# Expert rows in three pieces of 128, and part of the scan's products with C on GpSimd

## The chip, the cores and the metric

The kernel runs on one core of a Trainium2 chip. The metric is the device time of one execution in microseconds (us). The engines are TensorE (PE in the profile, its weight loads PEld), VectorE (DVE), ScalarE (ACT), GpSimd (POOL) and SyncE (SP), which only issues DMAs here.

## The reference

The input is x, 8 sequences of 512 tokens of width 128. Two layers follow, each of the form `x + s * silu(g)` on a normalised x: s comes from an attention-like branch, g from a mixture of experts. In layer 0, s is a Mamba block and g a top-2 mixture of 24 experts in 4 groups of 1024 tokens, each expert taking at most 86 tokens of a group, two matrices deep (128 to 512, layer norm, relu, 512 to 128). In layer 1, s is an attention with 8 heads and g a top-2 mixture of 128 experts. The change touches layer 0 only. Its scan, cut to what matters:

```
h = exp(dt*A) * h + dt * B * x          # per token, 256 channels x 16 states
y = sum over states of (h * C)          # then + x*D, * silu(z), out projection
disp = dispatch(tokens to experts)      # 24 experts x 4 groups x 86 places
h1 = disp @ W1 + b1 ; r = relu(layer_norm(combine(h1)))
out = combine(dispatch(r) @ W2 + b2)
```

## The kernel before, in words

The scan stage (`scan_stage`, about 120 to 800 us of the span) runs the scan and, beside it on the same engines, both expert matrices of layer 0 (`Moe0Experts`). There are 64 steps `i`: 8 sequences b, and in each 8 pairs q of states (q = i mod 8). A step handles two states j = 0, 1 of both channel halves h for 512 tokens.

Each engine has its own instruction stream, in program order, with semaphores between them. In step i:

- VectorE: `times_b(i,0)`, `times_c(i-1,0)`, `times_b(i,1)`, `times_c(i-1,1)`: four products of 128x1024, each of a tensor in SBUF (u, or the states `st`) with one row of B or C that TensorE has broadcast over all partitions into a PSUM bank. Then two scans (L672), one for each channel half, both inputs in SBUF. After the scans, in some steps: `split_rest` (q=0), `split_low` (q=1), four softplus operations (q=3 and 6, L617 to L623), and in q=1 `gate` between the products.
- TensorE: broadcasts the rows (L501) into the three banks of `p_bc`, used in rotation, so that a broadcast waits for whoever used the row three places earlier. It sums the states (`sum_states`, L532, 8 transposes that accumulate in PSUM), once after the product of state 0 and once after that of state 1. `times_b(i+1,0)` on VectorE waits for both sums of step i-1 (the semaphore `hc_used`), since it writes over those states (a ring of four).
- ScalarE: `decays`, four exponentials a step (L444), two for each channel half.

The experts' work is laid between these by slots: each stream is a Python generator, and `side_by_side` lets the scan's stream run to its next `yield`, then the experts' stream to its next. Before the change TensorE has 4 slots in a step (5 in uneven odd ones), ScalarE and VectorE 2. Slots carry three phases in order. In the first, an expert's token rows are gathered by GpSimd (`gather_x`, L1270, one indirect DMA for each group of 96 rows), turned by TensorE, multiplied by W1 (L1361, one piece of 96 rows to a slot), copied out by ScalarE (L1433, and L1423 for the turned rows) and stored. In the second, 16 units of two token tiles are gathered back, combined, normed and weighed; GpSimd's two operations of `weigh` (L1300, L1302) wait for the end of the scans of a chosen step. In the third, rows of r are gathered (L1310), turned (L1409), copied by ScalarE (L1539), multiplied by W2 (L1396) and stored. The pieces of one expert are its 4 groups, padded from 86 to 96 rows: 96 pieces in phases one and three each. GpSimd does not take part in the scan and its stream is not tied to the steps.

TensorE's slot waits for ScalarE's copy of the piece two before it, and ScalarE's slot waits for TensorE's piece of the same slot.

The routing ahead of the scan (`Routing0`) makes the table of rows with 64 small matmuls (L1047), one set for each group, for which VectorE waits (L1147).

Of the kernel before, what the change touches and what calls it, by code (L numbers as in the profile page):

```python
# [38 lines left out]
CP = 96  # L39

# [266 lines left out]
PE_SLOTS, ACT_SLOTS, DVE_SLOTS = 4, 2, 2  # L307

EVEN_FROM, EVEN_TO, FIRST_WINDOW = 22, 43, 26


def uneven(i):

    return not EVEN_FROM <= i < EVEN_TO


def scan_stage(nc, w, xT, z, spare, beside):
# [6 lines left out]
    with ExitStack() as ctx:  # L326
# [14 lines left out]
        st = s.sb("st", [P, RS, 2, L])  # L341
        p_bc = s.ps("p_bc", [P, 3, L])
# [20 lines left out]
        row_used = s.sem("row_used")  # L363
        hc_used = s.sem("hc_used")
# [9 lines left out]
        def b_row(i, j):  # L374

            return 4 * i + 2 * j

        def c_row(i, j):

            return 4 * i + 2 * j + 5  # L380

        rows_in_order = sorted([b_row(i, j) for i in range(STEPS) for j in range(2)] +
                               [c_row(i, j) for i in range(STEPS) for j in range(2)])

        def rows_to(k):

            return sum(1 for n in rows_in_order if n <= k)

        def scalar_steps(act):
# [8 lines left out]
            def copy_hi(b):  # L398
                act.wait_ge(xp_ready, b + 1)
                if b >= 2:  # L400
                    act.wait_ge(row_ready, rows_to(c_row(PAIRS * (b - 1) - 1, 1)))
                nc.scalar.activation(bc3[:, b % 2, :], p_x[0:96, :], ACT.Copy).then_inc(hi_copied, 1)
# [6 lines left out]
            def softplus_logs(b, h):  # L409
# [10 lines left out]
                nc.scalar.activation(logs[:, 1, :], logs[:, 0, :], ACT.Ln, bias=1.0).then_inc(ln_ready, 1)  # L420

# [29 lines left out]
            for i in range(STEPS):  # L451
# [11 lines left out]
                if i % 4 == 3 and uneven(i) or i == EVEN_FROM - 2:  # L463
                    yield
# [12 lines left out]
        def tensor_steps(pe):  # L477
# [20 lines left out]
            def broadcast(k, b, n):  # L498
                if rows_to(k - 3):
                    pe.wait_ge(row_used, rows_to(k - 3))  # L500
                nc.tensor.matmul(p_bc[:, k % 3, :], w["sel"][:, n * P:(n + 1) * P], bc3[:, b % 2, :], start=True,  # L501
                                 stop=True).then_inc(row_ready, 1)

            def broadcast_b(i, j):
# [3 lines left out]
                broadcast(b_row(i, j), b, 2 * q + j)  # L508

            def broadcast_c(i, j):  # L510
                b, q = divmod(i, PAIRS)
                broadcast(c_row(i, j), b, DS + 2 * q + j)
# [11 lines left out]
            def sum_states(i, j):  # L524
# [4 lines left out]
                pe.wait_ge(row_used, rows_to(c_row(i, j)))  # L529
# [26 lines left out]
            for i in range(STEPS):  # L556
                b, q = divmod(i, PAIRS)
                if i:
                    broadcast_c(i - 1, 1)
                if b + 1 < B:  # L560
# [19 lines left out]
                yield  # L580
                yield
                if i % 2 and uneven(i):
                    yield
                if i == EVEN_FROM - 2:
                    yield
                    yield
# [6 lines left out]
        def vector_steps(dve):  # L593
# [37 lines left out]
            def times_b(i, j):  # L631
                b, q = divmod(i, PAIRS)
                k = b_row(i, j)
                dve.wait_ge(row_ready, rows_to(k))
# [3 lines left out]
                if m >= RS and j == 0:  # L638
                    dve.wait_ge(hc_used, m - RS + 2)
                nc.vector.tensor_tensor(st[:, m % RS:m % RS + 2, j, :], u[:, b % 2, :, :],  # L640
                                        p_bc[:, k % 3, :].unsqueeze(1).broadcast_to([P, HALF, L]),
                                        ALU.mult).then_inc(row_used, 1)

            def times_c(i, j):
                m = 2 * i % RS
                k = c_row(i, j)
                dve.wait_ge(row_ready, rows_to(k))
                dve.wait_ge(scanned, 2 * i + 2)
                states = st[:, m:m + 2, j, :]
                nc.vector.tensor_tensor(states, states, p_bc[:, k % 3, :].unsqueeze(1).broadcast_to([P, HALF, L]),  # L650
# [6 lines left out]
            for i in range(STEPS):  # L657
# [7 lines left out]
                if i:  # L665
                    times_c(i - 1, 1)
                yield
                dve.wait_ge(row_used, rows_to(b_row(i, 1)))
# [14 lines left out]
                yield  # L683
                if i % 4 == 3 and uneven(i) or i == EVEN_FROM - 2:
                    yield
# [11 lines left out]

        @block.gpsimd
        def _(pool):
            for _ in beside.pool(pool):  # L700
                pass
# [263 lines left out]
class Routing0:  # L965
# [5 lines left out]
    def __init__(self, nc, ctx, w, r, xnT, p_n, spare):  # L971
# [21 lines left out]
        self.tabf = s.sb("tabf", [CP, HG, E0])  # L993
        self.p_l = s.ps("p_l", [P, 2, 512])
        self.p_t = s.ps("p_t", [CP, 512])
# [22 lines left out]
    def tensor(self, pe):  # L1018
# [24 lines left out]
        for h in range(HG):  # L1043
            for i in range(steps):
                t = i * HG + h
                for k in range(2):
                    ins = nc.tensor.matmul(p_t[:, h * 2 * E0:(h + 1) * 2 * E0], self.A[k][:, t, :],  # L1047
                                           self.R[k][:, t, :, :].rearrange("p a b -> p (a b)"),
                                           start=(i == 0 and k == 0), stop=(i == steps - 1 and k == 1))
# [25 lines left out]
    def vector(self, dve):  # L1075
# [53 lines left out]
        link(v.scalar_tensor_tensor(out=rows[:, :, :], in0=idx[:, :, :], scalar=float(CP), in1=loc[:, :, :],  # L1129
# [15 lines left out]
        pt = self.p_t[:, 0:HG * 2 * E0].rearrange("p (h a c) -> p h a c", h=HG, a=2)  # L1145
# [10 lines left out]
class Moe0Experts:  # L1156
# [13 lines left out]
    def __init__(self, nc, ctx, w, r, arena, xn_dram, W1, y1_dram, r_dram, W2, y2_dram, gathered):  # L1170
        self.nc, self.w, self.r = nc, w, r
        self.xn_rows = xn_dram.rearrange("p t d -> (p t) d")
        self.y1_dram, self.y1_rows = y1_dram, y1_dram.rearrange("h e c n -> (h e c) n")
# [9 lines left out]
        self.xg = first.sb("xg", [CP, 4, HG, D])  # L1183
        self.xgT = first.sb("xgT", [P, 2, HG * CP])
        self.out1 = first.sb("out1", [CP, 2, HG, HID])
# [3 lines left out]
        self.rg = second.sb("rg", [CP, 3, HG, HID])  # L1189
        self.rT = second.sb("rT", [P, 3, FC * CP])  # L1190
        self.out2 = second.sb("out2", [CP, 2, HG, D])
# [34 lines left out]
    def sync(self, sp):  # L1226

        for e in range(E0 + 1):
            if e < E0:
                if e >= 3:  # L1230
                    sp.wait_ge(self.piece_made, 5 * (e - 2))
                sp.dma_start(self.w1[:, e % 3, :], self.W1[e]).then_inc(self.w1_in[e % 3], 16)
            if e:
                f = e - 1
                sp.wait_ge(self.piece_read, 5 * (f + 1))
# [1527 lines left out]
```

## Time and profile before

| | |
|---|---|
| median of 3 runs | 1465.71 us (1464.28 to 1469.84) |
| span of the profiled execution, first to last instruction | 1465.0 us |
| TensorE, VectorE, ScalarE, GpSimd busy | 87%, 84%, 58%, 45% of the span |
| scan stage: scans, products with B, with C | 287.3, 154.3, 154.9 us of VectorE |
| indirect DMAs of phases one, two, three on GpSimd | 119.6, 90.9, 121.5 us |

The profiled execution's span is 0.7 us below the median of the runs; no other time of that execution is given. A row of a group names line, engine, operation, output and inputs, count, then busy time and mean nanoseconds of one, then the idle time of the engine ahead of it and what ended that. A row of a timeline gives start, duration, engine, line and operation; x2 means that two instructions in a row are merged. Records of one engine overlap a little at their ends, so the spacing of starts is the cost of one in a sequence.

### The profile page before, as it was taken

The numbers are of one execution on the slowest core, as the hardware profiler recorded it, in microseconds if no ns is written. First come the engines' busy times: TensorE is split into PE (matmuls) and PEld (weight loads), VectorE is DVE, ScalarE is ACT, GpSimd is POOL, SyncE is SP. The second block draws the span as 40 slices with busy tenths as digits, with TensorE's granted clock in tenths as the row PEclk, the third lists the DMA queues.
The fourth block names the chain that finished last, engine by engine and source line by source line (L and its number), as shares of the span: only waits on it lengthen the run. The fifth ranks groups of instructions, "written<-read, shape, count | busy, mean of one in ns | idle before, by whom it ended". The sixth has DMA issues, their size and how long they took to land. (4 is left out here: it accounts for less than half of the span.)

```text
span 1465.0 us, 21638 instructions
## 1 busy us (share of the span) xinstructions
PE 1277.5 (87%) x7304; PEld 888.3 (61%) x7304; DVE 1227.2 (84%) x2515; ACT 856.9 (58%) x2077; POOL 661.9 (45%) x612
## 2 busy tenths in 40 slices
PE   6977888897887976899897895599999999999997
PEld 5533444453433444788887774467676777777776
DVE  6678999998999899999997778869988555568877
ACT  5357757665798885556654658554464444444462
POOL 0018555605489855664751775339600322147300
PEclk9997999999999877999999898699999999999999
DMA  6003545545244422454552520300020233113201
GB/s 230 1 21 87 147 128 147 141 122 153 82 126 126 123 87 68 126 155 135 146 146 72 190 53 13 119 7 1 2 59 1 60 89 107 41 38 49 25 16 43
DMA packets 75747, 127.50 MB, mean 87 GB/s; under 512 B 11486, under 2 KB 38334, under 8 KB 75030
## 3 DMA queue, kind: packets, MB, share of 16 engines
q1 hardware_dynamic: 56182, 75.24, 17.0%
q0 software_dynamic: 19456, 50.88, 13.2%
q8 instruction: 59, 0.97, 0.3%
q14 instruction: 50, 0.41, 0.1%
HBM read 85.71 MB, written 40.37 MB: 86 GB/s over the span
## 5 line engine op out<-in xcount | busy, mean ns | idle before, releaser
L672 DVE TENSOR_TENSOR_SCAN sc_st<-sc_dA,sc_st 128x1024 f32<-128x1024 f32 x128 | 287.3, 2284 | 0.0
L2164 DVE COPY at_pT<-at_p_t 128x512 f32<-128x512 f32 (+1 forms) x192 | 109.0, 598 | 107.8 <-PE at_p_t L2046 107.4
L1270 POOL DMA_INDIRECT g_state<-xn_scratch,moe_tab x96 | 119.6, 1246 | 174.3 <-POOLq L99 102.4
L2059 PEld LDWEIGHTS at_p_o<-at_V,at_pT 128*128 128x128 f32 x1280 | 154.4, 194 | 31.1 <-issue 30.8
L444 ACT ACTIVATE sc_dA<-sc_dt,g_state 128x511 f32<-128x511 f32 x256 | 168.9, 710 | 7.2 <-DVE sc_st L672 5.3
L650 DVE TENSOR_TENSOR sc_st<-sc_st,sc_p_bc 128x1024 f32<-128x1024 f32 x128 | 154.9, 1211 | 13.4 <-PE sc_p_bc L501 13.2
L640 DVE TENSOR_TENSOR sc_st<-sc_u,sc_p_bc 128x1024 f32<-128x1024 f32 x128 | 154.3, 1206 | 6.6 <-PE sc_p_y L532 6.3
L1310 POOL DMA_INDIRECT g_state<-r_scratch,moe_tab x96 | 121.5, 1266 | 83.6 <-PE e_bank L1409 56.7
L2059 PE MATMUL at_p_o<-at_V,at_pT 128*128 128x128 f32 x1280 | 155.0, 277 | 3.6 <-DVE g_state L2153 3.6
L2026 PE MATMUL at_p_s<-att_xaT,at_qT 128*128 128x512 f32 (+3 forms) x512 | 150.7, 437 | 0.0
L501 PE MATMUL sc_p_bc<-sc_bc,mamba_sel 96*128 96x512 bf16 x256 | 104.9, 411 | 50.5 <-DVE sc_st L640 48.6
L2106 ACT ACTIVATE at_pr<-at_pr,at_nmx 128x512 f32<-128x512 f32 (+3 forms) x256 | 140.1, 551 | 13.3 <-DVE at_nmx L2138 13.1
L532 PEld LDWEIGHTS sc_p_y<-g_ident,sc_st 128*128 128x128 f32 x1024 | 126.9, 148 | 28.6 <-issue 16.3
L532 PE MATMUL sc_p_y<-g_ident,sc_st 128*128 128x128 f32 x1024 | 142.1, 285 | 0.8 <-DVE sc_st L650 0.7
L2094 ACT ACTIVATE at_V<-at_p_q 128x512 f32<-128x512 f32 x58 | 34.6, 596 | 163.3 <-PE at_p_q L2014 163.3
L2138 DVE CUSTOM_DVE_ANT_0 at_pr<-at_p_s,l_mask_wide 128x512 f32<-128x512 f32 (+3 forms) x256 | 111.4, 485 | 11.7 <-PE at_p_s L2026 11.4
L1280 POOL DMA_INDIRECT g_state<-y_scratch,moe_back x64 | 90.9, 1421 | 66.9 <-DMA y_scratch<-g_state 43.8
L2026 PEld LDWEIGHTS at_p_s<-att_xaT,at_qT 128*128 128x128 f32 x512 | 83.0, 191 | 52.8 <-issue 31.8
L1361 PE MATMUL e_bank<-g_state 128*96 128x512 f32 x192 | 100.7, 626 | 9.9 <-ACT g_state L1423 9.9
L2332 POOL DMA_INDIRECT f_xg<-xn_scratch,l_tab x32 | 30.3, 946 | 171.4 <-DVE l_tab L2540 85.1
L1396 PE MATMUL e_bank<-g_state 128*96 128x128 f32 x768 | 101.5, 275 | 4.4 <-ACT g_state L1530 4.0
L2046 PEld LDWEIGHTS at_p_t<-g_ident,at_pr 128*128 128x128 f32 x640 | 75.2, 141 | 39.3 <-DVE at_pT L2164 26.6
(304 smaller groups left out, 2615.0 us busy)
## 6 DMA issues: line engine op xcount, KB each, us to landing
y_scratch<-g_state SPq DMA_DIRECT2D x24, 768.0 KB, 5.2
g_state<-W SPq DMA_DIRECT2D x48, 256.0 KB, 5.5
r_scratch<-g_state SPq DMA_DIRECT2D x16, 512.0 KB, 3.6
y_scratch<-g_state SPq DMA_DIRECT2D x24, 192.0 KB, 2.8
xn_scratch<-g_state SPq DMA_DIRECT2D x16, 256.0 KB, 4.9
g_state<-x SPq DMA_DIRECT2D x4, 512.0 KB, 7.5
g_state<-xn_scratch SPq DMA_DIRECT2D x8, 256.0 KB, 5.2
g_state<-x SPq DMA_DIRECT2D x1, 2048.0 KB, 12.7
```

The costliest lines, as they stand in the source:

```text
L444: ins = nc.scalar.activation(dA[:, m % 4, j, 1:L], dt[:, b % 2, h, 1:L], ACT.Exp, scale=negA[:, h, 2 * q + j:2 * q + j + 1])
L532: ins = nc.tensor.matmul(p_y[:, t, h * P:(h + 1) * P], st[:, m + h, j, t * P:(t + 1) * P], w["ident"], is_transpose=True, start=False, sto ...
L640: nc.vector.tensor_tensor(st[:, m % RS:m % RS + 2, j, :], u[:, b % 2, :, :], p_bc[:, k % 3, :].unsqueeze(1).broadcast_to([P, HALF, L]), AL ...
L650: nc.vector.tensor_tensor(states, states, p_bc[:, k % 3, :].unsqueeze(1).broadcast_to([P, HALF, L]), ALU.mult).then_inc(row_used, 1)
L672: nc.vector.tensor_tensor_scan(st[:, m % RS, :, :].rearrange("p a b -> p (a b)"), dA[:, m % 4, :, :].rearrange("p a b -> p (a b)"), st[:, ...
L1270: nc.gpsimd.indirect_dma_start(out=self.xg[:, e % 4, h, :], out_offset=None, in_=self.xn_rows, in_offset=bass.IndirectOffsetOnAxis(ap=r.ta ...
L1310: nc.gpsimd.indirect_dma_start(out=self.rg[:, e % 3, h, :], out_offset=None, in_=self.r_rows, in_offset=bass.IndirectOffsetOnAxis(ap=r.tab ...
L2026: ins = nc.tensor.matmul(p_s[:, bank, c:c + K], qT[:, n % 3, i * P:(i + 1) * P], xaT[:, b, 0:K], start=True, stop=True)
L2059: ins = nc.tensor.matmul(p_o[:, i, :], pT[:, n % 2, bank, c + (i - j) * P:c + (i - j + 1) * P], V[:, b % 2, j, h * D:(h + 1) * D], start=( ...
L2106: ins = nc.scalar.activation(row, row, ACT.Exp, scale=-1.0, bias=nmx[:, n % 2, i:i + 1], accum_out=sums[:, n % 4, i:i + 1])
L2138: ins = v.tensor_tensor_reduce(out=pr[:, n % 3, bank, c:c + K], in0=p_s[:, bank, c:c + K], in1=w["mask_wide"][:, L - K:L], scale=1.0, scal ...
L2164: v.tensor_copy(pT[:, n % 2, part, 0:cols], p_t[:, PT_BANK[part], 0:cols]).then_inc(pT_ready, 1)
```

## The change

The experts' rows of all four groups (4 times 96) are laid out as one list of 384 and cut into three pieces of 128, so that every gather, turn, product and copy handles 128 rows and there are 72 pieces in each of phases one and three, not 96. The table is made by 112 small matmuls instead of 64, since the groups now straddle pieces. Every stream gets the same number of slots: 4 in odd steps and in steps 26 to 41, 3 in the other even steps.

In 31 of the 64 steps (`pooled(i)`: 0, 1, 3, 4, 6, 7, ... 24 and 42, 43, 45, 46, ... 61, two of every three, and none in steps 25 to 41, where GpSimd weighs), the product of state 1 with C leaves VectorE. TensorE broadcasts that C row a step earlier, ScalarE copies it to SBUF (`copy_c`, after its first two slots and the second pair of exponentials), and GpSimd multiplies (after the scans of that step). TensorE's sum of that state moves to the end of the next step, behind all slots. GpSimd's stream is tied to the steps now, through the same slots.

```
+CK = ROWS0 // P
-PE_SLOTS, ACT_SLOTS, DVE_SLOTS = 4, 2, 2
+UNIT_SLOTS = 4
+WIDE_FROM, WIDE_TO = 26, 42
+def slots(i):
+    return 4 if i % 2 or WIDE_FROM <= i < WIDE_TO else 3
+def pooled(i):
+    return i + 1 < B * DS // 2 and i + 1 not in WEIGH_STEPS and i % 3 != 2
...
+        for i in range(STEPS + 1):
+            if i < STEPS:
+                rows_in_order.append(("b", i, 0))
+            if i:
+                rows_in_order.append(("c", i - 1, 0))
+            if i < STEPS:
+                rows_in_order.append(("b", i, 1))
+            if i and not pooled(i - 1):
+                rows_in_order.append(("c", i - 1, 1))
+            if i < STEPS and pooled(i):
+                rows_in_order.append(("c", i, 1))
...  ScalarE
+            def copy_c(i):
+                n = pool_steps.index(i)
+                row = ("c", i, 1)
+                act.wait_ge(row_ready, place[row] + 1)
+                if n:
+                    act.wait_ge(c_weighed, n)
+                nc.scalar.activation(c_row[:, :], row_bank(row), ACT.Copy).then_inc(c_copied, 1)
...
                 yield
+                yield
                 if i + 1 < STEPS:
                     decays(i + 1, 1)
-                yield
+                if pooled(i):
+                    copy_c(i)
+                yield from [None] * (slots(i) - 2)
...  TensorE
+                at = place[row]
+                if at >= 3:
+                    last = rows_in_order[at - 3]
+                    if copied_row(last):
+                        pe.wait_ge(c_copied, pool_steps.index(last[1]) + 1)
+                    else:
+                        pe.wait_ge(row_used, used_on_vector(last))
...
-                if i:
+                if i and not pooled(i - 1):
                     broadcast_c(i - 1, 1)
+                if pooled(i):
+                    broadcast_c(i, 1)
...
-                if i:
+                if i and not pooled(i - 1):
                     sum_states(i - 1, 1)
                 if i + 1 < STEPS:
                     broadcast_b(i + 1, 1)
+                yield from [None] * (slots(i) - 2)
+                if i and pooled(i - 1):
+                    sum_states(i - 1, 1)
...  VectorE
-                if i:
+                if i and not pooled(i - 1):
                     times_c(i - 1, 1)
...  GpSimd
+        def pool_steps_of(pool):
+            for i in range(STEPS):
+                if i and pooled(i - 1):
+                    n = pool_steps.index(i - 1)
+                    m = 2 * (i - 1) % RS
+                    pool.wait_ge(c_copied, n + 1)
+                    pool.wait_ge(scanned, 2 * i)
+                    states = st[:, m:m + 2, 1, :]
+                    nc.gpsimd.tensor_tensor(states, states, c_row[:, :].unsqueeze(1).broadcast_to([P, HALF, L]),
+                                            ALU.mult).then_inc(c_weighed, 1)
+                yield from [None] * slots(i)
...  experts
-            for h in range(HG):
+            for h in range(CK):
                 nc.gpsimd.indirect_dma_start(
...
-            if 3 <= u < self.UNITS + 3:
-                weigh(u - 3)
+            if 4 <= u:
+                weigh(u - 4)
```

## Rows read from the trace of the kernel before

**Rows 1.** Stretches: us, then busy us (count) of PE, PEld, DVE, ACT, POOL, clock, DMA.

```profile
150.00:350.00 200.00, 166.06 (x703) 89.31 (x702) 191.41 (x144) 128.92 (x229) 91.53 (x76) 0.92 0.52 143
350.00:550.00 200.00, 168.41 (x585) 83.02 (x584) 189.67 (x189) 161.86 (x423) 143.61 (x81) 0.88 0.36 108
```

**Rows 2.** Groups of instructions by line: VectorE's products with C and with B.

```profile
L650 DVE TENSOR_TENSOR sc_st<-sc_st,sc_p_bc 128x1024 f32<-128x1024 f32 x128 | 154.9, 1211 | 13.4 <-PE sc_p_bc L501 13.2
L640 DVE TENSOR_TENSOR sc_st<-sc_u,sc_p_bc 128x1024 f32<-128x1024 f32 x128 | 154.3, 1206 | 6.6 <-PE sc_p_y L532 6.3
```

**Rows 3.** Timeline of all engines, 172 to 193 us: start, duration, what.

```profile
175.19 0.48 ACT L1423 ACTIVATE g_state<-e_bank 128x384 f32<-128x384 f32 x1
...
177.19 1.20 DVE L640 TENSOR_TENSOR sc_st<-sc_u,sc_p_bc 128x1024 f32<-128x1024 f32 x1
...
178.33 1.32 ACT L444 ACTIVATE sc_dA<-sc_dt,g_state 128x511 f32<-128x511 f32 x2
...
179.53 0.92 POOL L1270 DMA_INDIRECT g_state<-xn_scratch,moe_tab  x1 [0.30 <-issue]
179.55 1.06 ACT L1433 ACTIVATE g_state<-e_bank 96x512 f32<-96x512 f32 x2
...
181.70 4.47 DVE L672 TENSOR_TENSOR_SCAN sc_st<-sc_dA,sc_st 128x1024 f32<-128x1024 f32 x2
181.88 1.02 PE L1361 MATMUL e_bank<-g_state 128*96 128x512 f32 x2
...
182.74 1.03 PE L532 MATMUL sc_p_y<-g_ident,sc_st 128*128 128x128 f32 x8
183.00 0.60 ACT L1433 ACTIVATE g_state<-e_bank 96x512 f32<-96x512 f32 x1 [0.52 <-PE e_bank L1361]
183.61 0.38 PE L501 MATMUL sc_p_bc<-sc_bc,mamba_sel 96*128 96x512 bf16 x1
183.83 1.88 PE L1361 MATMUL e_bank<-g_state 128*96 128x512 f32 x4
...
185.01 1.88 POOL L1270 DMA_INDIRECT g_state<-xn_scratch,moe_tab  x1 [0.30 <-issue]
...
186.08 0.67 DVE L617 SCALAR_TENSOR_TENSOR g_state<-g_state,sc_logs 128x512 f32<-128x512 f32 x1
186.78 0.69 DVE L620 TENSOR_TENSOR g_state<-sc_logs,g_state 128x512 f32<-128x512 f32 x1
...
188.84 1.21 DVE L640 TENSOR_TENSOR sc_st<-sc_u,sc_p_bc 128x1024 f32<-128x1024 f32 x1
```

**Rows 4.** Timeline of all engines, 655 to 684 us, in phase three.

```profile
658.70 0.49 PE L1409 MATMUL e_bank<-g_ident,g_state 96*128 96x96 f32 x4
...
659.23 0.49 ACT L1539 ACTIVATE g_state<-e_bank 128x384 f32<-128x384 f32 x1 [0.45 <-PE e_bank L1409]
...
659.91 0.49 PE L1409 MATMUL e_bank<-g_ident,g_state 96*128 96x96 f32 x4
```

**Rows 5.** Timeline, 438 to 443 us: GpSimd's weighing runs into the scans.

```profile
440.44 2.35 POOL L1302 TENSOR_TENSOR g_state<-g_state,moe_ln_b 128x1024 f32<-128x1024 f32 x1
...
442.26 2.67 DVE L672 TENSOR_TENSOR_SCAN sc_st<-sc_dA,sc_st 128x1024 f32<-128x1024 f32 x1
```

**Rows 6.** Waits, 120 to 340 us: who waited for whom, us, times, longest.

```profile
DVE sc_st L640 <- PE sc_p_y L532: 2.0, 2, 1.6
```

**Rows 7.** Waits, 340 to 575 us, in phase two.

```profile
DVE sc_st L650 <- PE sc_p_bc L501: 10.3, 5, 5.9
...
DVE sc_st L640 <- PE sc_p_y L532: 4.2, 2, 2.9
```

**Rows 8.** Timeline of TensorE, 163 to 192 us: the first broadcast of a step, after idling.

```profile
169.55 0.39 PE L501 MATMUL sc_p_bc<-sc_bc,mamba_sel 96*128 96x512 bf16 x1 [2.23 <-DVE sc_st L640]
```

**Rows 9.** Stretches, TensorE alone: us, busy us (count), granted clock, DMA.

```profile
170.00:172.00 2.00, 2.00 (x4) 0.50 0.22 47
```

**Rows 10.** Timeline of TensorE, 68 to 76 us: the routing table's matmuls.

```profile
70.30 3.02 PE L1047 MATMUL r_p_t<-r_R,g_state 128*96 128x48 bf16 x64
```

More of the change, by code:

```diff
@@ L372, in scan_stage, with copied_row, used_on_vector, row_bank @@
         block = ctx.enter_context(nc.Block())
[L374 to L387, printed above, removed]
+        rows_in_order = []
+        for i in range(STEPS + 1):
[9 more added lines that the diff above has]
+                rows_in_order.append(("c", i, 1))
+        place = {row: n for n, row in enumerate(rows_in_order)}
+        pool_steps = [i for i in range(STEPS) if pooled(i)]
+        def copied_row(row):
+            return row[0] == "c" and row[2] == 1 and pooled(row[1])
+        def used_on_vector(row):
+            return sum(1 for r in rows_in_order[:place[row] + 1] if not copied_row(r))
+        def row_bank(row):
+            return p_bc[:, place[row] % 3, :]
         def scalar_steps(act):
@@ L632, in times_b @@
                 b, q = divmod(i, PAIRS)
-                k = b_row(i, j)
-                dve.wait_ge(row_ready, rows_to(k))
+                row = ("b", i, j)
+                dve.wait_ge(row_ready, place[row] + 1)
                 if q == 0 and j == 0:
@@ L682, in vector_steps @@
                         softplus(b + 1, (q - 3) // 3)
-                yield
-                if i % 4 == 3 and uneven(i) or i == EVEN_FROM - 2:
-                    yield
+                yield from [None] * (slots(i) - 2)
             times_c(STEPS - 1, 0)
@@ L1046, in tensor @@
                 for k in range(2):
-                    ins = nc.tensor.matmul(p_t[:, h * 2 * E0:(h + 1) * 2 * E0], self.A[k][:, t, :],
-                                           self.R[k][:, t, :, :].rearrange("p a b -> p (a b)"),
-                                           start=(i == 0 and k == 0), stop=(i == steps - 1 and k == 1))
+                    for first, end, piece, row in PLACES[h]:
+                        ins = nc.tensor.matmul(p_t[row:row + end - first, piece * 2 * E0:(piece + 1) * 2 * E0],
+                                               self.A[k][:, t, first:end],
+                                               self.R[k][:, t, :, :].rearrange("p a b -> p (a b)"),
+                                               start=(i == 0 and k == 0), stop=(i == steps - 1 and k == 1))
         ins.then_inc(self.table, 1)
@@ L1307, in gather_r @@
             if e >= 3:
-                pool.wait_ge(self.turned2, HG * (e - 2))
-            for h in range(HG):
+                pool.wait_ge(self.turned2, CK * (e - 2))
+            for h in range(CK):
                 nc.gpsimd.indirect_dma_start(
@@ L1318, in pool @@
             gather_x(e + self.AHEAD)
-            yield
+            yield from [None] * CK
         for i in range(2):
@@ L1360, in tensor @@
                     pe.wait_ge(self.piece_read, k - 1)
-                nc.tensor.matmul(bank[0:CP, k % 2, :], self.xgT[:, e % 2, h * CP:(h + 1) * CP],
+                nc.tensor.matmul(bank[:, k % 2, :], self.xgT[:, e % 2, h * P:(h + 1) * P],
                                  self.w1[:, e % 3, :], start=True, stop=True).then_inc(self.piece_made, 1)
-                if h == 3 and e + 1 < E0:
+                if h == CK - 1 and e + 1 < E0:
                     turn(e + 1)
                 yield
-        yield from [None] * PE_SLOTS
+        yield from [None] * UNIT_SLOTS
         for u in range(self.UNITS + 4):
-            for slot in range(PE_SLOTS):
+            for slot in range(UNIT_SLOTS):
                 t = 2 * u + slot
@@ L1414, in tensor @@
             yield
-        product(E0 * HG - 1)
+        product(E0 * CK - 1)
     def scalar(self, act):
@@ L1505, in scalar @@
                                              self.centred, 1)
+            yield
             yield
```

187 lines of the change are left out of this document (92 added, 95 removed).

## The prediction

> **What bounds the kernel now.** I read the busy time by stretches first. In the scan stage VectorE is busy 191.4 and 189.7 of 200 us, TensorE 166 and 168, GpSimd 92 and 144 [rows 1]: VectorE sets the pace, TensorE follows close, and the stages behind the scan can only shift with it. Then the groups by line: in the whole stage VectorE waits 13.4 + 6.6 = 20.0 us ahead of its products [rows 2]; 14.5 of that is in phase two (10.3 + 4.2) [rows 7], so 5.5 in phases one and three, 2.0 of it for sums in phase one [rows 6]. Then one step in the timeline. Four products take 4.51 us (177.19 to 181.70), 1.13 each; two scans 4.38 (to 186.08); a plain step is 8.9 us [rows 3]. A removed product is thus worth 1.13 us as long as nothing else is late.
>
> **What is removed.** 31 products: 31 x 1.13 = 35.0 us of VectorE.
>
> **TensorE's late sum: the term that decides.** Call T the start of a step's first product. Take a step whose own and whose preceding step's products are both moved (A, i mod 3 = 1); B (i mod 3 = 2) is the one after it, N (i mod 3 = 0) the one before it, in which VectorE still makes four. VectorE's next products need the sum of GpSimd's product, which now stands at the end of TensorE's step. VectorE itself is ready at T + 3 x 1.13 + 4.38 = T + 7.8.
>
> TensorE's order in A, with its costs: broadcast 0.22 (183.61 to 183.83), expert piece 0.86 (181.88 to 182.74), sum 0.87 (to 183.61) [rows 3]. The row for GpSimd goes out once the first product has freed its bank, T + 1.2; slot 0 ends at 2.3; the next B row waits for the second product, 2.4 to 2.6; the sum of state 0 ends at 3.5; the C row waits for the third product, 3.5 to 3.7; slot 1's piece starts at 3.7. The next broadcast now goes into the bank that ScalarE must first copy, and ScalarE copies it only behind slot 1's piece and two exponentials: piece to copy 1.12 (181.88 to 183.00), the copy 0.60, exponentials 1.22 (178.33 to 179.55) [rows 3], the new copy 0.60 (its row is not in the trace; the nearest, the expert copy out of PSUM, is), so 3.7 + 3.5 = 7.2. TensorE idles from 4.6 to 7.2. Then broadcast, slot 2, sum: 7.5, 8.3, 9.2, and 0.2 until it has drained. With 3 slots the sum is 1.6 us late, 1.8 with the turn that falls into slot 0. A with 4 slots has the turn in slot 2, and slot 3 waits for two copies of ScalarE (1.12 + 0.60 + 0.48 after slot 2's start at 7.5, so 9.7 [rows 3]), ends at 10.55, sum at 11.5: 3.7 late. In B no row is copied and TensorE ends near T + 7.7: nothing late. In N the sum of the step before stands where it stood (today it ends 183.77 - 177.19 = 6.6 after T [rows 3]), but TensorE runs into the next step.
>
> Phase one: A steps 4, 10, 16 cost 1.8 each, 1, 7, 13 cost 3.7 each: 16.5. Extra TensorE work in front of slot 1 at 1 (a sequence's start, 16 transposes, two sums' worth, 1.75), at 7 and by overrun at 16 (a projection, two pieces' worth, 1.7 each) and 13 (0.4), less short VectorE operations at 1 and 16 (1.3): +4.2. Step 19 is covered by softplus. Sum 20.7.
>
> Phase three: a slot costs 1.21 (658.70 to 659.91) [rows 4], 1.32 with a third more columns to turn. The same chain: slot 1 at 4.1; ScalarE starts 0.53 (659.23) + 0.11 later, copy 0.60, exponentials 1.22, copy 0.60: 7.2; with 3 slots the sum ends 2.0 late, with 4 slots 3.4. N overruns by 0.9 (3 slots) or 2.2 (4), and the second pushes the 3-slot A after it to 3.0. Steps 52, 58: 6.0; 49, 55, 61: 10.2, +1.4 for the extra work in 49 and 61; B of 4 slots (47, 53, 59) 0.9 each and 1.7 for a projection at 47: 4.4. Steps 43 and 46 are covered by softplus. Sum 22.0. Bounds of the two sums together: none, if something lets ScalarE copy early, to 42.7 plus half-clock stretches (below).
>
> **GpSimd beside softplus.** GpSimd's product has no row; the weighing of the same shape takes 2.35 us [rows 5]. It starts when the scans end. In plain steps it then runs beside products with one input in SBUF and is over by T + 2.6, before the next scans at 3.4: no cost. Its gathers take 0.92 us in that stretch and end about 0.8 after a scan when they meet one (185.01 + 1.88 against 186.08) [rows 3]; three of them put the product at T + 0.9 at worst, still over by 3.3; a second batch in a step, four times a phase, might push a scan by up to 1 us (0 to 8 us in all; I take 0). In q = 3 and 6 softplus comes right behind the scans, and most of its operations read two SBUF tensors. The row for this is a scan that lasts 2.67 instead of 2.23 because GpSimd's weighing, which began first, ends 0.53 into it [rows 5]. The first softplus operation (186.08) begins before GpSimd can; GpSimd gets in ahead of the second (186.78) and VectorE waits 2.3. Eight moved products stand there (3, 6, 19, 22, 43, 46, 51, 54): 8 x 2.3 = 18.4; at least 0, if VectorE's four operations keep GpSimd out.
> The Trainium skill, "SBUF — State Buffer", section "Who interferes with whom", says that a VectorE instruction with two SBUF inputs and a GpSimd instruction that reads SBUF exclude each other for the whole of the one that started first. By that rule the 18.4 us stand; without it the sum would be 18.4 lower. The trace agrees as far as the 2.67 us scan goes; no run shows it at softplus.
>
> **The rest.** The three pieces shed work that is mostly cover: 24 of 96 pieces in two phases on TensorE, ScalarE and GpSimd. VectorE's 5.5 us of waits in phases one and three are inside the new ones above: -5.5. In phase two the gathers back now go out a step ahead of their unit, so that TensorE should wait less; of VectorE's 14.5 us [rows 7] I take -8 (0 to -14.5), since GpSimd still runs into scans there [rows 5]. Ahead of the scan, 48 more table matmuls at 3.02/64 us [rows 10] are 2.3, on VectorE's path: +2.3 (0 to 2.3). ScalarE's 31 copies (19 us) replace 24 expert copies of the same size; cover, but for the place named above.
>
> **Sum**, against the span of 1465.0: -35.0 + 20.7 + 22.0 + 18.4 - 5.5 - 8 + 2.3 = +14.9, so 1480 us; the median of the runs lies 0.7 above the span, within the rounding.
>
> **Rivals.**
> Faster: TensorE's late sum is hidden, because ScalarE copies the row early enough or the sum meets slack that I don't see. It decides at T + 7.8: a sum that ends before it costs nothing. Then 1480 - 42.7 = 1437. For it: TensorE waits in every step now, 2.23 us in one [rows 8], and sheds a slot. Against: the order in the streams leaves no choice, and the durations are rows. Half of it gives 1458.
> Even: GpSimd is kept out through softplus. 1480 - 18.4 = 1462, some 2 us more as sums at 19, 22, 43, 46 come to light: 1464. For it: gathers there don't lengthen softplus (186.08 to 188.84 is the usual pace [rows 3]). Against: they read little.
> Much slower: TensorE's new idle time (2.6 us in A, about 2 in N) brings half clock. After 2.23 us of idling [rows 8] the clock is 0.50, the lower level of 1.2 GHz [rows 9]. Behind the wait an A step still has 2 to 2.8 us of TensorE work; doubled in the ten uncovered ones, +22: 1502. Against: many such gaps today leave the mean at 0.92 [rows 1].
> That the change moves fewer products than its name says is a matter of the list: 31 of 64, and the sum counts those.
>
> **Chances.** Forecast (1473 to 1492) 0.43, much slower 0.15, even 0.17, faster 0.25. The range 1445 to 1505 leaves out about half of the faster case and little of the slowest. About 0.5% (7.3 us) is what a measurement tells from no change: slower 0.58, same 0.17, faster 0.25. The likeliest case's own range is 1473 to 1492.
>
> **What would show it.** In the changed profile: VectorE idle ahead of its first product with B, waiting for TensorE's sums, 1.5 to 4 us in some ten A steps and hardly in B and N; TensorE idle about 2.5 us ahead of a broadcast, released by ScalarE's row copy; the softplus operation of eight steps 2.3 us longer; GpSimd's products 2.4 us each, starting at the end of the scans. I am wrong if VectorE's waits in phases one and three stay near 5 us, if softplus keeps its pace, or if the scans grow by more than a few us in all.

## The result and the profile after

The changed kernel takes 1582.0 us (median of 4 runs, 1579.1 to 1583.2), the kernel before 1466.3 (1464.3 to 1469.8): a ratio of 1.078, 95% interval 1.076 to 1.080. I had forecast slower, 1480 us, at most 1505. The direction was right, the size was not: +116 us where I had +15. The profiled execution spans 1581.4 us (1465.0 before); TensorE's mean granted clock is 0.899 (0.939 before).

I cut the span at the start of VectorE's first product with B in steps 0, 22, 42 and 63. After (timeline of VectorE: start, duration, what):

```profile
135.91 2.35 DVE L690 TENSOR_TENSOR sc_st<-sc_u,sc_p_bc 128x1024 f32<-128x1024 f32 x2
...
399.37 1.19 DVE L690 TENSOR_TENSOR sc_st<-sc_u,sc_p_bc 128x1024 f32<-128x1024 f32 x1
...
676.56 1.22 DVE L690 TENSOR_TENSOR sc_st<-sc_u,sc_p_bc 128x1024 f32<-128x1024 f32 x1
...
899.13 1.20 DVE L690 TENSOR_TENSOR sc_st<-sc_u,sc_p_bc 128x1024 f32<-128x1024 f32 x1
```

The same starts in every kernel of this study, in us (one profiled execution each; rows 11 and 12 are one kernel twice and differ by up to 3.6 us in a stretch, so I read nothing smaller from single stretches):

| kernel | ahead of step 0 | steps 0-21 | steps 22-41 | steps 42-62 | span |
|---|---|---|---|---|---|
| before | 120.9 | 217.1 | 241.9 | 204.2 | 1465.0 |
| after | 135.9 | 263.5 | 277.2 | 222.6 | 1581.4 |
| 1 no product moved | 135.3 | 215.9 | 282.9 | 202.5 | 1520.4 |
| 2 row copied early | 134.3 | 233.9 | 282.7 | 211.9 | 1544.4 |
| 3 sum early | 134.8 | 229.6 | 285.3 | 200.0 | 1532.4 |
| 4 weighing first | 136.0 | 260.6 | 251.4 | 224.4 | 1554.7 |
| 5 = 2 + 3 | 135.0 | 214.1 | 287.4 | 201.1 | 1519.5 |
| 6 = 5 + 4 + wide table | 124.1 | 214.9 | 256.6 | 201.1 | 1478.4 |
| 7 = 5 + wide table + units on steps | 123.8 | 214.8 | 253.9 | 202.5 | 1474.6 |
| 8 = 1 + 4 + wide table | 124.8 | 215.2 | 256.3 | 203.3 | 1479.9 |
| 9 = 7 + product after softplus | 125.1 | 209.8 | 251.7 | 198.3 | 1461.5 |
| 10 = 9 + weighed a unit sooner | 124.7 | 212.9 | 250.1 | 201.0 | 1465.6 |
| 11 = 10 + weighing first | 124.9 | 210.9 | 241.9 | 201.0 | 1455.2 |
| 12 = 11 again | 122.5 | 209.3 | 245.5 | 201.0 | 1454.9 |

So the 116 us are four losses: 15.0 ahead of the scan, 46.4 in phase one, 35.3 in phase two, 18.4 in phase three, and 1.3 behind step 63. VectorE in the two stretches of [rows 1]:

```profile
150.00:350.00 200.00, 147.14 (x550) 81.12 (x550) 148.54 (x108) 104.49 (x185) 108.89 (x74) 0.85 0.39 120
350.00:550.00 200.00, 153.92 (x543) 78.67 (x542) 179.56 (x146) 126.03 (x305) 108.95 (x68) 0.87 0.36 107
```

It was busy 191.4 and 189.7 us and is 148.5 and 179.6: it no longer sets the pace. What it does, by line, 130 to 905 us (these answer to [rows 2]; the scans and three softplus operations are added):

```profile
L723 DVE TENSOR_TENSOR_SCAN sc_st<-sc_dA,sc_st 128x1024 f32<-128x1024 f32 x127 | 315.1, 2521 | 1.0
L690 DVE TENSOR_TENSOR sc_st<-sc_u,sc_p_bc 128x1024 f32<-128x1024 f32 x128 | 155.1, 1212 | 111.0 <-PE sc_p_y L584 109.6 <-PE sc_p_bc L550 1.3
L700 DVE TENSOR_TENSOR sc_st<-sc_st,sc_p_bc 128x1024 f32<-128x1024 f32 x95 | 115.2, 1213 | 0.1
...
L670 DVE TENSOR_TENSOR g_state<-sc_logs,g_state 128x512 f32<-128x512 f32 x15 | 15.1, 1010 | 0.5
L673 DVE TENSOR_TENSOR sc_u<-sc_dt,mamba_xT 128x512 f32<-128x512 f32 x16 | 13.1, 819 | 0.5
L671 DVE TENSOR_TENSOR sc_dt<-sc_dt,g_state 128x512 f32<-128x512 f32 x15 | 12.4, 827 | 0.5
```

The products with C fell by what was moved. The first row has 127 of the 128 scans; all of them take 317.3 us (287.3 before). In exchange VectorE waits 111.0 us ahead of its products with B (6.6 before), nearly all for TensorE's sums. Who waited for whom in phase one, 136 to 400 us (us, times, longest):

```profile
POOL sc_st L755 <- ACT g_state L463: 116.3, 11, 17.4
DVE sc_st L690 <- PE sc_p_y L584: 58.4, 11, 13.7
...
PE sc_p_bc L550 <- ACT g_state L463: 28.9, 14, 2.5
```

L463 is ScalarE's row copy: GpSimd waits for it ahead of its products, TensorE ahead of the broadcast that reuses the bank. Step 7, an A step, with T = 221.14 (timeline of all engines):

```profile
222.63 2.48 PE L528 MATMUL sc_p_x<-mamba_xT,mamba_xproj_T 128*104 128x512 f32 x4
...
224.65 4.47 DVE L723 TENSOR_TENSOR_SCAN sc_st<-sc_dA,sc_st 128x1024 f32<-128x1024 f32 x2
224.91 1.91 PE L1422 MATMUL e_bank<-g_state 128*128 128x512 f32 x2
...
228.22 1.02 PE L1422 MATMUL e_bank<-g_state 128*128 128x512 f32 x2
229.27 0.60 ACT L1495 ACTIVATE g_state<-e_bank 128x512 f32<-128x512 f32 x1 [1.75 <-PE e_bank L1422]
229.77 1.32 ACT L487 ACTIVATE sc_dA<-sc_dt,g_state 128x511 f32<-128x511 f32 x2
230.99 0.58 ACT L463 ACTIVATE g_state<-sc_p_bc 128x512 f32<-128x512 f32 x1
...
231.63 0.39 PE L550 MATMUL sc_p_bc<-sc_bc,mamba_sel 96*128 96x512 bf16 x1 [2.39 <-ACT g_state L463]
...
234.91 1.04 PE L584 MATMUL sc_p_y<-g_ident,sc_st 128*128 128x128 f32 x8
...
236.08 1.22 DVE L690 TENSOR_TENSOR sc_st<-sc_u,sc_p_bc 128x1024 f32<-128x1024 f32 x1 [6.96 <-PE sc_p_y L584]
```

Read it from the bottom: VectorE, ready at 229.12, waits 6.96 us for the sum at 234.91. That sum is of step 6, whose product GpSimd had finished before T; it stands at the end of TensorE's stream, behind the broadcast at 231.63, which waited 2.39 us for the copy at 230.99, which stood behind the expert copy and two exponentials. This is the chain of the prediction, to the instruction. The prediction had this sum 5.4 us late (3.7 and 1.7 for the projection). What it lacks: the piece at 224.91 lasts 1.91 us instead of 0.86 to 1.02. TensorE was granted a clock of 0.50 there, the lower of its two levels (stretch, TensorE alone: us, busy us and count, granted clock, DMA):

```profile
224.00:227.00 3.00, 3.00 (x5) 0.50 0.16 45
```

Phase two, 602 to 616 us:

```profile
603.74 0.94 POOL L1342 DMA_INDIRECT g_state<-y_scratch,moe_back  x1 [1.81 <-PE e_bank L1442]
...
605.94 2.38 POOL L1362 TENSOR_TENSOR g_state<-g_state,moe_ln_w 128x1024 f32<-128x1024 f32 x1
...
606.54 8.23 DVE L723 TENSOR_TENSOR_SCAN sc_st<-sc_dA,sc_st 128x1024 f32<-128x1024 f32 x2
...
608.40 4.22 POOL L1364 TENSOR_TENSOR g_state<-g_state,moe_ln_b 128x1024 f32<-128x1024 f32 x1
...
612.65 1.06 ACT L1556 ACTIVATE g_state<-g_state 128x1024 f32<-128x1024 f32 x1 [5.16 <-POOL g_state L1364]
```

The gathers wait for TensorE's pieces, the weighing stands behind the gathers (as it did before the change), begins 0.6 us before the scans, and two scans take 8.23 us instead of 4.45; ScalarE waits 5.16 us for the weighing, and its later operations, softplus among them, start that much later.

Ahead of the scan, the table (timeline of TensorE), which took 3.02 us for 64 matmuls [rows 10]:

```profile
69.36 15.55 PE L1108 MATMUL r_p_t<-r_R,g_state 128*96 128x48 bf16 x112
```

### The profile page after: what moved, and what is told of

The parts are those of the page before. It is cut to its first block and busy times, and to the rows that moved or that the text cites. A ratio compares the mean times of both kernels' runs of the same rounds, so it can differ in the third digit from the quotient of the medians.

```text
span 1581.4 us, 20955 instructions
## 1 busy us (share of the span) xinstructions
PE 1308.7 (83%) x6992; PEld 901.5 (57%) x6992; DVE 1235.5 (78%) x2484; ACT 855.5 (54%) x2060; POOL 689.9 (44%) x595
## 5 line engine op out<-in xcount | busy, mean ns | idle before, releaser
L723 DVE TENSOR_TENSOR_SCAN sc_st<-sc_dA,sc_st 128x1024 f32<-128x1024 f32 x128 | 317.3, 2519 | 1.0
L690 DVE TENSOR_TENSOR sc_st<-sc_u,sc_p_bc 128x1024 f32<-128x1024 f32 x128 | 155.1, 1212 | 111.0 <-PE sc_p_y L584 109.6
L584 PEld LDWEIGHTS sc_p_y<-g_ident,sc_st 128*128 128x128 f32 x1024 | 141.2, 161 | 46.3 <-issue 29.6
L584 PE MATMUL sc_p_y<-g_ident,sc_st 128*128 128x128 f32 x1024 | 157.6, 305 | 7.5 <-DVE sc_st L700 7.4
L1332 POOL DMA_INDIRECT g_state<-xn_scratch,moe_tab x72 | 93.7, 1302 | 136.7 <-POOLq L105 117.0
L1372 POOL DMA_INDIRECT g_state<-r_scratch,moe_tab x72 | 100.4, 1395 | 81.4 <-PE e_bank L1470 61.3
L550 PEld LDWEIGHTS sc_p_bc<-sc_bc,mamba_sel 96*128 96x128 bf16 x256 | 27.3, 107 | 186.0 <-DVE sc_st L690 88.4
L755 POOL TENSOR_TENSOR sc_st<-sc_st,g_state 128x1024 f32<-128x1024 f32 x31 | 73.9, 2385 | 133.5 <-ACT g_state L463 122.5
L700 DVE TENSOR_TENSOR sc_st<-sc_st,sc_p_bc 128x1024 f32<-128x1024 f32 x97 | 117.6, 1213 | 0.2
L1342 POOL DMA_INDIRECT g_state<-y_scratch,moe_back x64 | 78.1, 1221 | 70.5 <-PE e_bank L1442 43.5
L1495 ACT ACTIVATE g_state<-e_bank 128x512 f32<-128x512 f32 x72 | 42.5, 595 | 119.2 <-PE e_bank L1422 119.0
```

Of the source, the lines that this page charges most:

```text
L550: nc.tensor.matmul(row_bank(row), w["sel"][:, n * P:(n + 1) * P], bc3[:, b % 2, :], start=True, stop=True).then_inc(row_ready, 1)
L584: ins = nc.tensor.matmul(p_y[:, t, h * P:(h + 1) * P], st[:, m + h, j, t * P:(t + 1) * P], w["ident"], is_transpose=True, start=False, sto ...
L700: nc.vector.tensor_tensor(states, states, row_bank(row).unsqueeze(1).broadcast_to([P, HALF, L]), ALU.mult).then_inc(row_used, 1)
L723: nc.vector.tensor_tensor_scan(st[:, m % RS, :, :].rearrange("p a b -> p (a b)"), dA[:, m % 4, :, :].rearrange("p a b -> p (a b)"), st[:, ...
L1372: nc.gpsimd.indirect_dma_start(out=self.rg[:, e % 3, h, :], out_offset=None, in_=self.r_rows, in_offset=bass.IndirectOffsetOnAxis(ap=r.tab ...
```

## The experiments

**1. No product moved.** Is it the moved products, or the pieces and slots?

```diff
 def pooled(i):
-    return i + 1 < B * DS // 2 and i + 1 not in WEIGH_STEPS and i % 3 != 2
+    return False
```

> No product moves to GpSimd and no row is copied; pieces of 128, slots and units stay as in the changed kernel. Theory A (the moved products' late sums cost phases one and three): steps 0 to 21 fall from 263.5 us to about 217 and steps 42 to 63 from 222.6 to about 204, VectorE's waits ahead of its first product fall from 110 us to under 35, span 1581 - 46 - 18 = 1517. Rival (pieces of 128 rows and the new slots cost it): the span stays above 1565. The front (135.9) and phase two (277.2) stay as they are in both.

1522.2 us. Phases one and three return to 215.9 and 202.5; the front and phase two stay. All of the loss in phases one and three comes with the moved products; the pieces of 128 cost nothing there. The other two losses, at the front and in phase two, have nothing to do with the moved products.

**2 and 3. The copy early, the sum early.**

```diff
 # 2, ScalarE's step
                 yield
+                if pooled(i):
+                    copy_c(i)
                 yield
                 if i + 1 < STEPS:
                     decays(i + 1, 1)
-                if pooled(i):
-                    copy_c(i)
```

```diff
 # 3, TensorE's step, second slot
-                if i and not pooled(i - 1):
+                if i:
                     sum_states(i - 1, 1)
...
-                if i and pooled(i - 1):
-                    sum_states(i - 1, 1)
```

> ScalarE copies the row ahead of the second slot's work instead of behind it and two exponentials. If the copy's place is what makes the sums late, TensorE's waits for the copy (48.9 us of idling) fall under 15 and VectorE's 110 us of waits to 50 or less: 1520 to 1540. If it is the sum's own place, behind the last slots, that counts, VectorE still waits 2 to 4 us in each of ten steps or more a phase, and the gain is under 25: above 1555.

> TensorE sums the moved product where it sums the others, ahead of the broadcast that waits for ScalarE's copy; the copy stays late. If the place of the sum decides, VectorE's waits fall from 110 us to about 30 and the time to 1500 to 1520. If TensorE's idling ahead of the broadcast decides by itself (it pushes the slots and the next step's broadcasts), TensorE still idles 40 us or more for the copy, the waits move to the next step's rows, and the time stays above 1550.

1546.2 and 1534.2 us. Neither is where one cause alone would put it. The early copy takes TensorE's waits for it from 48.9 us to 5.2, yet VectorE still waits 69.6 us in the scan stage, and its softplus operations take 8.7 us more in all than in the changed kernel; the early sum takes VectorE's to 52.1 with TensorE still idling 33.0 for the copy. Of the 64.8 us that phases one and three had lost, the one gives back 40.3 and the other 56.5, more than all of it between them: they are two links of one chain.

**4. The weighing ahead of the gathers in phase two.**

```diff
-            gather_y(u + 1)
             if 4 <= u:
                 weigh(u - 4)
+            gather_y(u + 1)
```

> GpSimd's order in phase two only: the weighing of a unit ahead of the gathers of a later one, which wait for TensorE's pieces. If the weighing runs into the scans because it stands behind those gathers, the scan pairs of 5.5 to 8.3 us return to about 4.5, the 42 us that ScalarE waits for the weighing shrink, and steps 22 to 41 take 242 to 250 us instead of 277: 1546 to 1555. If TensorE's waits there come from ScalarE's softplus behind the later slots, the scans shorten (about 25 us) but the steps stay at 265 or more: above 1568.

1556.6 us, steps 22 to 41 at 251.4, both some 1.5 us above the range expected. VectorE's scans there (groups by line, 400 to 655 us) are nearly at their own pace of 2.23 us:

```profile
L723 DVE TENSOR_TENSOR_SCAN sc_st<-sc_dA,sc_st 128x1024 f32<-128x1024 f32 x42 | 94.4, 2289 | 0.0
```

The weighing behind the gathers was 26 of the 35 us. VectorE's waits for sums in phase two stay (23.6 us; 21.7 after).

**5. Copy and sum early.**

> Both edits of the two runs before: ScalarE's row copy ahead of the second slot, and the moved product's sum in the place of the others. Front and phase two stay as they are. If the two orders together are what phases one and three lose, VectorE's waits there fall under 12 us, and steps 0 to 21 take 200 to 212 us, steps 42 to 63 190 to 198, less than the 217 and 204 of the kernel before: 1506 to 1522 in all. If the lower clock and the 128-row pieces hold TensorE back by themselves, steps 0 to 21 stay above 217.

1521.4 us. VectorE's waits for sums in steps 0 to 21 are 5.7 us (58.4 after). Phases one and three are 3 us shorter than before the change, no more than the scatter; I had expected 5 to 17 and 6 to 14. Phase one's TensorE alone (stretch: us, busy us and count, granted clock, DMA), after and here:

```profile
136.00:400.00 264.00, 191.16 (x722) 0.84 0.37 116
```

```profile
135.00:349.00 214.00, 170.82 (x722) 0.90 0.45 140
```

722 recorded instructions in both took 20.3 us less. The mean granted clock rose from 0.84 to 0.90: the idling ahead of the late copies had brought TensorE more time at the lower level of 1.2 GHz, instead of 2.4, on top of the idling itself.

**6. The routing table with full matmuls,** beside edits 2 to 4.

```diff
-   for first, end, piece, row in PLACES[h]:
-       ins = nc.tensor.matmul(p_t[row:row + end - first, piece * 2 * E0:(piece + 1) * 2 * E0],
-                              self.A[k][:, t, first:end], ...
+   ins = nc.tensor.matmul(p_t[:, h * 2 * E0:(h + 1) * 2 * E0], self.A[k][:, t, :], ...
 # A: one-hots of (group_base + loc) mod 128, 128 wide; VectorE then copies the
 # four groups' rows into the three pieces (6 copies)
```

> Copy and sum early, the weighing ahead of the gathers in phase two, and a routing table made by 64 matmuls of 128 columns each (one-hots of 128 places, the four groups' parts put together by VectorE) in place of 112 of 32, 64 and 96. If it is the 112 narrow matmuls that hold up the front (15.6 us where the 64 took 3.0), the first step starts at 123 to 126 us instead of 136, with the granted clock at 1.0 where it was 0.5; if the clock falls there for another reason, it starts at 133 or later. With phases of 205, 251 and 194: 1465 to 1485.

1480.2 us, the first step at 124.1:

```profile
72.96 2.74 PE L1105 MATMUL r_p_t<-r_R,g_state 128*128 128x48 bf16 x64 [3.20 <-DVE r_S L1196]
```

The 112 narrow matmuls were the front's loss. Half of the expectation missed: TensorE had idled 3.2 us here, the clock from 72 to 76 us is 0.62, and the table is still quick. So the clock was the smaller part. After, three stretches of its line L1108 (count, shortest, median and longest in ns, first and last start, columns loaded):

```profile
L1108 PE MATMUL r_p_t<-r_R,g_state x16: 186/203/203, 69.4 to 70.0; 128*96 128x48 bf16 x16
...
L1108 PE MATMUL r_p_t<-r_R,g_state x27: 197/203/210, 70.0 to 73.5; 128*32 128x48 bf16 x13, 128*64 128x48 bf16 x13, 128*96 128x48 bf16 x1
...
L1108 PE MATMUL r_p_t<-r_R,g_state x57: 219/223/249, 74.8 to 83.9; 128*32 128x48 bf16 x29, 128*64 128x48 bf16 x28
```

Each of them overlaps its neighbours, so the spacing of starts is what counts. The first 16, 96 columns each as before the change, follow each other every 45 ns; those of 32 and 64 columns in turn every 133 ns, with the clock still granted 1.00 up to 73 us, and every 163 ns behind that. Here it is 43 (2.74/64). The narrow ones have fewer columns and also alternate between rows of the result; which of the two slows them no run separates. The phases are longer than I expected (214.9, 256.6 and 201.1 instead of 205, 251 and 194); runs 8 to 11 look into that.

**7. Units on steps.**

```diff
-UNIT_SLOTS = 4
-WIDE_FROM, WIDE_TO = 26, 42
+UNIT_SLOTS, LEAD = 4, 5          # LEAD: the gap ahead of the first unit
+WIDE_FROM, WIDE_TO = 22, 42
```

> As the run with four edits, but phase two mended in another way: GpSimd keeps its order (gathers, then the weighing), and each unit starts in the first slot of a step, as before the change, instead of the second; all steps from 22 to 41 have four slots. If the shift of the units by a slot is what brings the weighing into the scans, steps 22 to 41 take 240 to 250 us and the scan pairs are at 4.45 to 4.9; if GpSimd's order alone does it, they stay above 270.

1476.4 us, steps 22 to 41 at 253.9, 4 us above the range expected, with GpSimd's order unchanged. Either mend frees most of the scans: those of steps 22 to 41 take 95.5 us here, 91.5 in run 6 and 126.9 in run 5. So it takes both, the gathers ahead of the weighing and the unit's shift by a slot, to push the weighing into the scans.

**8. The same without moved products.**

> No product moves to GpSimd; the weighing stands ahead of the gathers and the table is made by 64 full matmuls. What this takes longer than the run with four edits is what the moved products are worth once nothing is late. By the pieces alone I expect phases of 216, 251 and 203 and a first step at 124: about 1480; if the moved products are worth the 1.13 us each that a product took, the run with four edits is 25 to 30 us faster than this one, if GpSimd's products cost VectorE as much as they save, the two agree within 8.

1481.8 us: 1.5 more than run 6, which is within the scatter of single runs. With the orders mended and next to nothing late in phases one and three, 31 moved products are still worth nothing that single runs can show. Where their 35 us went shows in VectorE's groups, 120 to 800 us, run 6 and then run 8:

```profile
L719 DVE TENSOR_TENSOR_SCAN sc_st<-sc_dA,sc_st 128x1024 f32<-128x1024 f32 x126 | 287.9, 2326 | 1.0
L686 DVE TENSOR_TENSOR sc_st<-sc_u,sc_p_bc 128x1024 f32<-128x1024 f32 x128 | 154.9, 1211 | 37.9 <-PE sc_p_y L582 37.5
...
L666 DVE TENSOR_TENSOR g_state<-sc_logs,g_state 128x512 f32<-128x512 f32 x15 | 21.2, 1417 | 0.5
L669 DVE TENSOR_TENSOR sc_u<-sc_dt,mamba_xT 128x512 f32<-128x512 f32 x15 | 15.0, 999 | 0.5
L663 DVE SCALAR_TENSOR_TENSOR g_state<-g_state,sc_logs 128x512 f32<-128x512 f32 x15 | 12.1, 808 | 2.7 <-ACT g_state L452 2.7
```

```profile
L721 DVE TENSOR_TENSOR_SCAN sc_st<-sc_dA,sc_st 128x1024 f32<-128x1024 f32 x126 | 282.0, 2280 | 0.0
L688 DVE TENSOR_TENSOR sc_st<-sc_u,sc_p_bc 128x1024 f32<-128x1024 f32 x127 | 153.6, 1210 | 32.3 <-PE sc_p_y L582 31.9
...
L668 DVE TENSOR_TENSOR g_state<-sc_logs,g_state 128x512 f32<-128x512 f32 x15 | 10.4, 692 | 0.5
L671 DVE TENSOR_TENSOR sc_u<-sc_dt,mamba_xT 128x512 f32<-128x512 f32 x15 | 10.4, 692 | 0.5
L665 DVE SCALAR_TENSOR_TENSOR g_state<-g_state,sc_logs 128x512 f32<-128x512 f32 x15 | 10.0, 668 | 2.7 <-ACT g_state L452 2.7
```

Beside the moved products softplus costs 17.5 us more (10.8 + 4.6 + 2.1), the scans 5.9, the waits 5.6: 29.0 of the 35.

**9. The product behind softplus.**

```diff
                     pool.wait_ge(scanned, 2 * i)
+                    b, q = divmod(i - 1, PAIRS)
+                    if b + 1 < B and q in (3, 6):
+                        pool.wait_ge(u_ready, 2 * (b + 1) + (q - 3) // 3 + 1)
```

> As the run with the units on the steps (1476.4), and GpSimd's product of a step with softplus waits until softplus is over. There the softplus operations took 54.3 us in all, 13 more than without moved products. If GpSimd's product keeps VectorE's softplus waiting, they return to about 41 and the time falls by 11 to 16 us: 1460 to 1466. If the product then runs into the next scans, or its sum is late for the step after, the gain is lost there and the time stays at 1470 or more.

1463.3 us, 13.1 less. Of this 10.9 us are the operation that GpSimd had held, in run 7 and here:

```profile
L666 DVE TENSOR_TENSOR g_state<-sc_logs,g_state 128x512 f32<-128x512 f32 x16 | 22.0, 1374 | 0.5
```

```profile
L666 DVE TENSOR_TENSOR g_state<-sc_logs,g_state 128x512 f32<-128x512 f32 x16 | 11.1, 694 | 0.5
```

**10 to 12. Phase two once more, and the best version.** Run 10 has weigh(u - 3) in place of weigh(u - 4), so that GpSimd weighs in steps 25 to 40 and step 40's product moves in place of step 24's; run 11 also has the order of run 4; run 12 times run 11's kernel.

> As the run before it, and a unit is weighed one unit earlier (three after its own, not four), so that ScalarE's last operation on it need not wait in the same step for GpSimd. If that same-step chain (weighing, ScalarE, TensorE's pieces) is what keeps phase two at 254 us against 242, steps 22 to 41 take 240 to 246 us and the time is 1448 to 1455; if TensorE's waits for ScalarE's softplus keep it there, it stays within 4 us of the run before it.

> As the run before it, and the weighing ahead of the gathers as well. The scans of phase two should all be at 4.5 us; 3 to 6 us less in steps 22 to 41 than without, unless the gathers, behind the weighing now, land late for TensorE's pieces: then up to 10 us more.

> The kernel of the run before, timed against the kernel before the change. If the 9 us between the two single times are real, the ratio is 0.992 to 0.996 and its interval lies below 1; if single times scatter that far, the interval holds 1.

Run 10: 1467.5 us, 4.2 more than run 9; phase two gains 1.6, less than the scatter, so the chain that I suspected was not what held it. Run 11: 1457.0 us, phase two at 241.9 as in the kernel before; the same kernel again, in run 12, has 245.5 there. Run 12: 1457.1 us (median of 6, 1453.0 to 1461.0) against 1468.0 for the kernel before (median of 11), ratio 0.992, interval 0.990 to 0.994. This version is 0.8% faster than the kernel before the change.

## Why the prediction was wrong

The direction and most of the mechanism held. What failed: the gathers of phase two (-8), which had the wrong sign; the late sums of phase one (20.7), which were mis-sized; the scans (0); and the routing table (2.3), mis-sized. Its terms, laid out by stage (the prediction's own numbers; products by the steps that lose them, 14, 3 and 14):

| stage | predicted | measured |
|---|---|---|
| ahead of step 0 | +2.3 | +15.0 |
| phase one: -15.8 products, +20.7 sums, +6.9 softplus, -2.0 waits | +9.8 | +46.4 |
| phase two: -3.4 products, +2.3 softplus, -8 gathers | -9.1 | +35.3 |
| phase three: -15.8 products, +22.0 sums, +9.2 softplus, -3.5 waits (the rest of 5.5) | +11.9 | +18.4 |

VectorE's rows, cut at the same starts, give what the terms measured in phases one, two and three: its waits ahead of products grew by 57.1, 7.2 and 27.3 us, its scans by 0.9, 26.7 and 2.3, softplus by 2.0, 4.4 and 2.3.

**Phase two: the step failed in sign.** "In phase two the gathers back now go out a step ahead of their unit, so that TensorE should wait less", -8. I looked at what the gathers give TensorE, not at what stands behind them on GpSimd. There they wait 43.5 us for TensorE's pieces (6.8 before), and the weighing behind them runs into the scans. The C rows for which VectorE had waited 10.3 us [rows 7] do come on time now, but it waits 21.7 us for sums where it waited 4.2. This is the largest miss, 44 us; run 4 takes back 26 by an exchange of two lines, and in runs 11 and 12 phase two is where it was before, within the scatter.

**Phase one: right mechanism, wrong size.** VectorE waits 58.4 us for sums where I had 20.7. The steps behind A steps 1 to 19 wait 13.7, 3.3, 7.0, 5.7, 8.2, 6.5 and 4.9 us (49.3). Two things were missing. The lower clock, my rival "much slower" at 15%, came together with the forecast instead of in its place: run 5, without the late copies and sums, has 20.3 us less of TensorE time. And I priced each A step as if TensorE entered it on time, but N steps wait for a row copy too (in phase one it starts 9 to 14 us after T in all but one of them), and hand their lateness on; I had it in the text as "overruns" and priced only those into steps 13 and 16. Step 19 was not covered by softplus, either. How the excess divides between the two no run shows; these waits are 27.2 us in run 2, 20.6 in run 3 and 5.7 in run 5, so they go only when the late copy and the late sum are both gone.

**Phase three: close.** The waits for sums are 29.5 us against 22.0; the granted clock there is 0.92.

**Softplus: right, but hidden in this kernel.** I had +18.4; after shows +8.9 (15.1 + 13.1 + 12.4 less 46 x 0.69), because in five of the eight steps (3, 19, 46, 51 and 54) the late copy kept GpSimd's product away until softplus was over. Where a product does meet softplus, in steps 6, 22 and 43, it happens as priced; in step 6:

```profile
217.37 2.58 POOL L755 TENSOR_TENSOR sc_st<-sc_st,g_state 128x1024 f32<-128x1024 f32 x1 [9.03 <-ACT g_state L463]
...
217.77 2.72 DVE L671 TENSOR_TENSOR sc_dt<-sc_dt,g_state 128x512 f32<-128x512 f32 x1
```

The operation takes 2.72 instead of 0.69 us and ends 0.54 us after the product. With the copy early the term measures 17.5 (run 6 against 8). The wait of run 9 takes 10.9 us out of softplus; the other 2.2 of its 13.1 us are scatter as far as I can tell (3.0 lie behind step 63, where the edit changes nothing). By the rule that I drew on (the Trainium skill, "SBUF — State Buffer", section "Who interferes with whom") one of the two waits for the whole of the other; the trace agrees in these rows.

**The routing table: the term was mis-sized.** I took 48 more matmuls at 3.02/64 us each. But 96 of the 112 are narrow and take 133 ns each at the full clock, 163 at the lower level that follows (run 6); 15.55 - 3.02 = 12.5 us, and the convolution's eight matmuls behind them take 5.57 instead of 3.60.

**Scans and GpSimd's product: taken as 0.** In the changed kernel that is nearly so: outside phase two the scans grew by 3.2 us. With the copy early it is not: "three of them put the product at T + 0.9 at worst" holds only where the gathers are ready to go. In run 11 the first of three gathers in step 46 waits 5.99 us for TensorE, the product goes behind them and into the scans (timeline; GpSimd and VectorE's scan):

```profile
615.67 0.94 POOL L1383 DMA_INDIRECT g_state<-r_scratch,moe_tab  x1 [5.99 <-PE e_bank L1481]
...
618.36 6.60 DVE L719 TENSOR_TENSOR_SCAN sc_st<-sc_dA,sc_st 128x1024 f32<-128x1024 f32 x2
...
619.12 3.69 POOL L754 TENSOR_TENSOR sc_st<-sc_st,g_state 128x1024 f32<-128x1024 f32 x1
```

**What was right:** the 35 us of removed products, the chain from the late copy to the late sum, B steps of 7.9 us where nothing is late, and that the forecast's waits would fall on the products with B. Of my three signs of being wrong, two pointed to a faster kernel; the third came true: the scans grew from 287.3 to 317.3 us, 26.7 of it in phase two, under the weighing and not under the moved products.

**Open.** The products moved in phases one and three are worth 31.6 us; the best version keeps 6.6 of it in run 11 and 8.2 in run 12, against run 8. In run 11 the scans of these phases take 12.7 us more than in run 8 (eight pairs are 0.8 to 2.2 us longer), VectorE's waits 6.6 and softplus 2.1, which leaves some 4, within the scatter. Phase two's remaining waits for sums, 17 us in run 11 and 22 in run 12 (4.2 before), I have not traced. Not all that the best version gains comes from the moved products: of the 9.8 us that run 11's span is shorter than before, 4.2 lie behind step 63. There the last product with W2 starts 8.3 us after the start of step 63 (16.5 before; 8.3 too in every kernel with run 7's edit), and the stage behind the scan begins 3.3 us sooner. No run has run 11's kernel without moved products.

## What to carry to other kernels

An in-order queue prices a new instruction by everything ahead of it and everything behind it: walk both directions for each engine that the edit touches, also where an edit only shifts a stage by a slot. A wait that idles TensorE is paid twice where its clock then falls, and lateness is handed on to the next step: here waits that added up to 2 to 5 us came to 3 to 14. Work moved to an idle engine is worth its time only while it stays clear of the operations that it holds up on the engine it left: here 31 products of 1.13 us came to 1.5 us, until the product was kept out of softplus, and more than half of what is left still goes to longer scans and to waits.

## What the runs showed that I had not expected

- Narrow matmuls of a table, 32 and 64 columns in turn into changing rows: 133 ns each with the clock granted 1.00; 96 columns took 45 ns each in the same table, 64 of 128 columns 43. While the narrow ones ran, TensorE not idling once by the profile, the granted clock fell from 1.00 to 0.50 (stretches of L1108: us, busy us and count of PE and PEld, clock, DMA; the counts take in matmuls that reach over an edge):

```profile
71.00:72.00 1.00, 1.00 (x9) 0.75 (x8) 1.00 0.00 0
...
74.00:75.00 1.00, 1.00 (x9) 0.70 (x8) 0.50 0.00 0
```

- Two GpSimd operations of 2.4 us that meet a pair of scans lengthen the pair from 4.45 to 8.23 us, and the second of them from 2.36 to 4.22.
